# Two attention layers with mixtures of experts: PSUM banks dealt by head, and the products of an image's step spread anew

## The reference

```python
x = x + tanh(g_xattn[0]) * L0_xattn(layernorm(x), ctx, Wq, bq, Wk, bk, Wv, bv, Wo, bo)
x = x + tanh(g_ffn[0])   * L0_ffn(layernorm(x), ...)      # 32 experts, 4 per row, and a shared one
x = x + tanh(g_xattn[1]) * L1_xattn(layernorm(x), ctx, ctx, gamma)
x = x + tanh(g_ffn[1])   * L1_ffn(layernorm(x), ...)      # 8 experts, 2 per row, and shared ones

def L0_xattn(x, c, ...):        # 16 heads of 8 channels; layer 1 has 8 heads of 16
    q, k, v = Wq x + bq, Wk c + bk, Wv c + bv
    p = softmax(einsum('bhkt,bhks->bhts', q, k) / sqrt(8), axis=-1)
    return Wo einsum('bhts,bhks->bhkt', p, v) + bo
```

## Time and profile before

| | |
|---|---|
| median of 3 runs | 734.75 us (732.73 to 735.25) |
| the profiled execution | 734.11 us, span 732.3 us |
| TensorE matmuls busy | 652.4 us, 89% of the span |
| VectorE busy | 517.6 us, 71% |
| ScalarE busy | 370.8 us, 51% |
| GpSimd busy | 355.1 us, 48% |
| mean granted clock of TensorE | 0.974 |
| layer 0 attention, roughly | 19 to 253 us of the span |
| layer 1 attention, roughly | 385 to 548 us |

### The profile page before, as it was taken

The page is one execution under the profiler, slowest core; times in us unless marked ns, Lnnn a source line. Parts: engine busy times, 40 slices in busy tenths (PEclk is TensorE's granted clock), DMA queues, the critical chain, the costliest instruction groups (busy, mean ns, idle before and its releaser), DMA issues.

```text
span 732.3 us, 13733 instructions
## 1 busy us (share of the span) xinstructions
PE 652.4 (89%) x4737; PEld 343.0 (47%) x4738; DVE 517.6 (71%) x1238; ACT 370.8 (51%) x616; POOL 355.1 (48%) x409
## 2 busy tenths in 40 slices
PE   3789999999999989989864778999989899999997
PEld 1233333333333336677541334445543367777754
DVE  3788989888889479946336898999873863333336
ACT  2147788788777634445330565666642203444430
POOL 3845646656431110077276886762010036777735
PEclk9999999999999999999995799999999999999999
DMA  6945545565633194044653667975317412222228
GB/s 149 211 108 137 147 124 140 151 177 148 171 95 88 46 308 82 6 150 139 192 166 96 190 202 194 231 208 157 109 40 235 118 33 70 87 89 88 68 95 282
DMA packets 110151, 101.12 MB, mean 138 GB/s; under 512 B 26344, under 2 KB 95629, under 8 KB 109611
## 3 DMA queue, kind: packets, MB, share of 16 engines
q1 hardware_dynamic: 100259, 80.52, 39.6%
q0 software_dynamic: 8352, 18.74, 9.1%
q10 hardware_dynamic: 1472, 0.99, 0.7%
HBM read 58.49 MB, written 24.40 MB: 113 GB/s over the span
## 4 chain that ended last, share of the span: by engine, by line
PE 58%; DVE 15%; issue 8%; POOL 7%; DMA 7%; SPq 3%; ACT 2%; POOLq 0%; ACTq 0%; DVEq 0%
PE O L478 12%; PE S L433 11%; PE ST L1569 6%; DVE mx L597 4%; POOL spare L305 4%; PE ST L441 3%; DMA QS<-mxT 3%; PE M L1586 2%; PE S L1586 2%; PE M L527 2%; PE M L520 2%; PE ST L1481 2%; SPq L170 1%; DMA PX<-xn,TI 1%; PE M L503 1%
## 5 line engine op out<-in xcount | busy, mean ns | idle before, releaser
L597 DVE TENSOR_REDUCE mx<-S 128x2 f32<-128x512 f32 x384 | 251.2, 684 | 37.0 <-PE S L433 35.1
L353 ACT ACTIVATE PX<-ST 128x1024 f32<-128x1024 f32 x192 | 196.1, 1023 | 95.3 <-PE ST L441 91.7
L433 PE MATMUL S<-QS 62*128 62x256 bf16 (+1 forms) x768 | 151.2, 292 | 37.0 <-DVE mx L597 29.0
L441 PE MATMUL ST<-QS 64*128 64x256 bf16 (+1 forms) x768 | 140.7, 277 | 4.5 <-DMA QS<-mxT 4.5
L478 PE MATMUL O<-PX,VA 128*32 128x256 f32 x1536 | 122.7, 392 | 0.1
L433 PEld LDWEIGHTS S<-QS 62*128 62x128 bf16 (+1 forms) x768 | 48.5, 97 | 153.9 <-DVE mx L597 98.7
L305 POOL DMA_INDIRECT spare<-ye,GI x64 | 68.2, 1066 | 26.4 <-issue 12.6
L1687 POOL DMA_INDIRECT PX<-xn,TI x39 | 39.8, 1020 | 52.6 <-DVE K1n L1881 37.2
L441 PEld LDWEIGHTS ST<-QS 64*128 64x128 bf16 (+1 forms) x768 | 53.8, 96 | 19.0 <-issue 9.0
L810 POOL DMA_INDIRECT PX<-xn,TI x32 | 34.1, 1065 | 53.6 <-DVE spare L1196 44.1
L284 POOL TENSOR_TENSOR X<-X,rd 128x256 f32<-128x256 f32 x16 | 11.6, 726 | 86.0 <-ACT rd L363 86.0
(11 more groups left out here) (299 smaller groups left out, 1119.9 us busy)
## 6 DMA issues: line engine op xcount, KB each, us to landing
QS<-QKs SPq DMA_DIRECT2D x93, 128.0 KB
QS<-keys SPq DMA_DIRECT2D x16, 512.0 KB, 5.5
keys<-spare SPq DMA_DIRECT2D x96, 64.0 KB, 2.3
QS<-QKs SPq DMA_DIRECT2D x93, 64.0 KB
EGU<-in_ew SPq DMA_DIRECT2D x16, 256.0 KB, 4.4
xn<-spare SPq DMA_DIRECT2D x8, 512.0 KB, 10.9
ye<-QKc SPq DMA_DIRECT2D x32, 128.0 KB, 2.1
VA<-in_val SPq DMA_DIRECT2D x16, 256.0 KB, 3.7
```

Of the source, the lines that this page charges most:

```text
L353: e.activation(M["PX"][pair % 4][:, :], M["ST"][pair % 2][:, :], ACT.Exp, scale=A.scale).then_inc(A.exp, 1)
L433: got = e.matmul(M["S"][n % 2][:, 256 * a:256 * a + 256], QS[:, 0, 128 * a:128 * a + 128], QS[:, 1, :], start=True, stop=True)
L441: got = e.matmul(M["ST"][(NP * t + k // 2) % 2][:, 512 * u + 256 * a:512 * u + 256 * a + 256], QS[:, 1, 128 * a:128 * a + 128], QS[:, 0, : ...
L597: e.tensor_reduce(M["mx"][b % 2][:, :, A.row_of_max(head)], M["S"][n % 2][:, :].rearrange("p (a s) -> p a s", a=2), AX.X, ALU.max, negate= ...
```

## The change

Four things change together.

- PSUM: three banks S, three banks ST, each for one head; O and M1 stay. The waits follow: a score for a maximum may be three heads ahead instead of two, and exponentials are taken head by head.
- Layer 0, values: the two halves of a quad stand in one block, behind heads 4 (the last quad of the image before), 7, 11 and 14.
- Layer 0, other products and copies: projections behind head 2 (was 1), maxima's transposes behind 6 (was 5); on VectorE statistics at 2 (was 0), reciprocals at 4 (was 0), context's sum at 9 (was 10), normalisation at 12 (was 13); on ScalarE the copies move to the matching heads.
- In layer 1 the products stay in place; only banks and the exponentials' heads change.

```diff
+QK_OUT, MX_OUT, OS_FIRST, OS_LAST = 3, 6, 11, 4
...
-            w.wait_ge(A.st, A.NP * (b2 - U + 1))
+            w.wait_ge(A.st, H * (b2 - U + 1))
...
-    def exponentials(b, m):
-        pair = NP * b + m
-        w.wait_ge(A.st, pair + 1)
-
-        w.wait_ge(A.pv, pair // 2 - 1)
-        e.activation(M["PX"][pair % 4][:, :], M["ST"][pair % 2][:, :], ACT.Exp, scale=A.scale).then_inc(A.exp, 1)
+    def exponentials(b, k):
+        n = H * b + k
+        w.wait_ge(A.st, n + 1)
+
+        w.wait_ge(A.pv, n // 4 - 1)
+        e.activation(M["PX"][n // 2 % 4][:, 512 * (n % 2):512 * (n % 2) + 512], M["ST"][n % 3][:, :], ACT.Exp,
+                     scale=A.scale).then_inc(A.exp, 1)
...
-                if m == 0 and within(b0):
+                if k == QK_OUT and within(b0):
...
-                if m == 1 and within(b4):
+                if k == OS_LAST and within(b4):
                     values_out(b4, 1)
-                if m == 2 and within(b2):
+                if k == MX_OUT and within(b2):
                     rows_out(b2)
-                if m == 5 and within(b3):
+                if k == OS_FIRST and within(b3):
                     values_out(b3, 0)
...
-            w.wait_ge(A.max, n - 1)
+            w.wait_ge(A.max, n - 2)
...
-            w.wait_ge(A.exp, NP * t + k // 2 - 1)
+            w.wait_ge(A.exp, H * t + k - 2)
...
-                if k == 1 and within(b0):
+                if k == 2 and within(b0):
                     projections(b0)
-                if k in (2, 3) and within(b4):
-                    values(b4, 3, k - 2)
-                if k == 5 and within(b2):
+                if k == 4 and within(b4):
+                    values(b4, 3, 0, 1)
+                if k == 6 and within(b2):
                     maxima(b2)
-                if k in (6, 7, 10, 11, 14, 15) and within(b3):
-                    values(b3, k // 4 - 1, k % 2)
+                if k in (7, 11, 14) and within(b3):
+                    values(b3, (7, 11, 14).index(k), 0, 1)
...
-                if k == 0 and within(bn):
+                if k == (0 if t < 0 else 2) and within(bn):
                     statistics(bn)
...
-                if k == 0 and within(b5):
+                if k == 4 and within(b5):
                     reciprocals(b5)
-                if k == 10 and within(b2):
+                if k == 9 and within(b2):
...
-                if k == 13 and within(b5):
+                if k == 12 and within(b5):
                     normalized(b5)
...
-    S, ST = [ps("S0"), ps("S1")], [ps(f"ST{n}", 1024) for n in range(2)]
+    S, ST = [ps(f"S{n}") for n in range(3)], [ps(f"ST{n}") for n in range(3)]
     M["S"], M["ST"], M["O"], M["M1"] = S, ST, ps("O"), ps("M1")
-    M["BK"] = [S[0][:, :], S[1][:, :]] + [ST[n][:, 512 * k:512 * k + 512] for n in range(2) for k in range(2)]
-    M["BK"] += [M["O"][:, :], M["M1"][:, :]]
+    M["BK"] = [bank[:, :] for bank in S + ST + [M["O"], M["M1"]]]
```

More of the change, by code:

```diff
@@ L364, in attention_act @@
                          bias=M["bog"][:, 0:1], scale=M["tg"][:, 0:1]).then_inc(A.yb, 1)
-        for m in range(NP):
+        for k in range(H):
             if within(b3):
-                exponentials(b3, m)
+                exponentials(b3, k)
             if A.first:
-                if m == 0 and within(b0):
+                if k == QK_OUT and within(b0):
                     w.wait_ge(A.kp, b0 + 1)
@@ L376, in attention_act @@
                 if b0 == 0:
-                    if m == 1:
+                    if k == 4:
                         w.wait_ge(A.kc, 1)
                         e.activation(part_of(S, 0), Q, ACT.Copy).then_inc(A.cut0, 1)
-                    if m == 2:
+                    if k == 5:
                         w.wait_ge(A.res1, 1)
                         e.activation(part_of(S, 1), Q, ACT.Copy).then_inc(A.cut1, 1)
-                    if m == 3:
+                    if k == 6:
                         w.wait_ge(A.res2, 1)
-                        for k in range(3, 6):
-                            spread(e, A, M, 0, k)
-                if m == 1 and within(b4):
+                        for i in range(3, 6):
+                            spread(e, A, M, 0, i)
+                if k == OS_LAST and within(b4):
                     values_out(b4, 1)
-                if m == 2 and within(b2):
+                if k == MX_OUT and within(b2):
                     rows_out(b2)
-                if m == 5 and within(b3):
+                if k == OS_FIRST and within(b3):
                     values_out(b3, 0)
             else:
-                if m == 1:
+                if k == 3:
                     if within(b2):
@@ L402, in attention_act @@
                         e.activation(part_of(S, 0), Q, ACT.Copy).then_inc(A.cut0, 1)
-                if m == 2 and within(b0):
+                if k == 5 and within(b0):
                     w.wait_ge(A.res1, b0 + 1)
                     e.activation(part_of(S, 1), Q, ACT.Copy).then_inc(A.cut1, 1)
-                if m == 3 and b0 == 0:
+                if k == 7 and b0 == 0:
                     w.wait_ge(A.res2, 1)
-                    for k in range(3, 6):
-                        spread(e, A, M, 0, k)
-            meanwhile(t, m)
+                    for i in range(3, 6):
+                        spread(e, A, M, 0, i)
+            if k % 2:
+                meanwhile(t, k // 2)
 def attention_pe(e, w, A, M, meanwhile=lambda t, k: None):
-    H, NQ, NP = A.H, A.NQ, A.NP
+    H, NQ = A.H, A.NQ
     M1, QSs = M["M1"], M["QS" + A.name]
@@ L432, in for_maximum @@
             QS = QSs[A.stack(c)][row:row + A.K - 2, g, :, :]
[L433 removed]
+            got = e.matmul(M["S"][n % 3][:, 256 * a:256 * a + 256], QS[:, 0, 128 * a:128 * a + 128], QS[:, 1, :],
                            start=True, stop=True)
@@ L439, in for_exponential @@
             row, g = A.where(k)
-            QS, u = QSs[A.stack(t)][row:row + A.K, g, :, :], k % 2
-            got = e.matmul(M["ST"][(NP * t + k // 2) % 2][:, 512 * u + 256 * a:512 * u + 256 * a + 256],
+            QS = QSs[A.stack(t)][row:row + A.K, g, :, :]
+            got = e.matmul(M["ST"][(H * t + k) % 3][:, 256 * a:256 * a + 256],
                            QS[:, 1, 128 * a:128 * a + 128], QS[:, 0, :], start=True, stop=True)
-            if a and u:
+            if a:
                 got.then_inc(A.st, 1)
@@ L473, in values @@
         w.wait_ge(A.oe, n // 2)
-        w.wait_ge(A.exp, NP * b + 2 * quad + 2)
+        w.wait_ge(A.exp, H * b + 4 * quad + 4)
         for a in halves:
             for u in range(4):
-                pair = NP * b + 2 * quad + u // 2
+                pair = (H * b + 4 * quad + u) // 2
                 got = e.matmul(M["O"][32 * u:32 * u + 32, 256 * (quad % 2):256 * (quad % 2) + 256],
```

18 lines of the change are left out of this document (9 added, 9 removed).

## The result

The changed kernel takes 743.66 us (median of 4 runs, 741.79 to 746.62) where the kernel before takes 733.74 on the same chip (4 runs, 732.62 to 735.25): a ratio of 1.0152, interval 1.0118 to 1.0187. It is 9.9 us slower.

A forecast was written before the change was run, and what follows sets the result against it. The prediction took TensorE as the tightest engine, SyncE's queue just behind, and a loop through Cb to bind after the change: 734.1 - 1.5 + 13.0 - 5.0 - 1.0 = 739.6 us, range 733 to 747.

The forecast's parts named there:

- The loop through Cb: Layer 0, L505 to reciprocal, rT, SyncE's issues and Cb's landing: 14.8 us a round against 13.36, +13.0 over nine rounds.
- The queue does not bind (718): Rival, layer 0: the wait for rT does not hold Cb, TensorE's 12.4 sets the round; 718 us, chance 0.10.
- TensorE's own round: Layer 0: TensorE's work per image falls from 13.36 to 12.4 us through the blocks and the third bank.
- The banks: Layer 0, steady part: three banks for the maxima save 0.2 us an image of TensorE's waits.
- the blocks: Layer 0: a quad's values in one block instead of two save TensorE 0.76 us an image.
- Before the loop: Warm-up: with three banks TensorE bounds some 20 heads at 0.62 us each; 1.5 us saved.
- Exponentials by head, hidden: ScalarE, layer 0: +1.2 us an image, load 10.5 to 11.7, hidden by TensorE's 12.4; nothing taken.
- Behind the loop, -5.0: Last L505 to the end of layer 0's values, without Cb: blocks save 3.7, waits for maxima 1.3, together 5.0 us.
- Layer 1, -1.0: Layer 1, values not merged: the third bank saves 1.0 us, bounds 0 and 3.
- The clock falls in the new waits (746): Rival: TensorE's 2.4 us wait each round lowers the clock, some 0.7 a round, +6, 746 us; chance 0.11.
- The gains outweigh (733 to 737): Rival, no change: a loop of 14.4 costs 9.4, gains of 3 in layer 1 and 6 behind it; chance 0.12.

The follow-up runs named there:

- e1: The changed kernel with the reciprocals put back from behind head 4's maximum to behind head 0's: 726.47 us.
- e9: The kernel before with one edit, the next image's Cb issued ahead of the six stores of keys: 731.16 us.
- e5: The changed kernel with the reciprocals back behind head 0 and Cb issued ahead of the stores of keys: 717.55 us.
- e6: e5 with two of the six stores of keys issued by ScalarE instead of SyncE: 709.78 us.
- e4: The kernel before with only the new banks (three S, three ST) and exponentials by head, everything else where it was: 727.71 us.
- e10: e6 with the reciprocals moved back behind head 4, as the change has them: 729.86 us.
- e3: The changed kernel, reciprocals still behind head 4, with the next image's Cb issued ahead of the six stores of keys: 728.28 us.
- e11: The changed kernel with two of the six stores of keys issued by ScalarE, Cb in its old place: 731.37 us.
- e8: e3 with rT issued behind dn and on instead of between the parts of the spread: 726.48 us.
- e2: The kernel before with only the reciprocals moved, from behind head 0's maximum to behind head 4's: 770.62 us.
- e12: e10 with two buffers OS in layer 0, so a copy waits for the on<-OS of the image before the last: 718.12 us.
- e7: e4 with Cb issued ahead of the stores of keys: 720.21 us.

## Why the prediction was right, and where it was wrong

**The loop through Cb: right in place and size.** Forecast 14.8 us a round and +13.0; measured 14.88 and +13.7. L505 to the reciprocal was forecast at 0.52 + 0.43 + 1.20 + 0.35 = 2.50 and measured 2.61. SyncE needed 9.3 to 10.4 for a forecast of 9.8. The wait for Cb was to be "some 20 in all" and is 20.0. e1 shows that the one line makes it (17.2 us), and e9 that the kernel before was not held by the queue. The page of the Trainium skill that was set against it (DMA: Bandwidth & Descriptors, "Issuing engines are not separate DMA queues") has the sequencer's time as usually small. No trace here agrees: an issue takes some 0.60 us beside a landing of 2.1 to 2.3, 19 of them fill 11.5 us of each of SyncE's rounds, and moving two of them to ScalarE brought 7.8 us (e5 to e6).

**The queue does not bind (718): excluded** by the same runs. Even with the reciprocal at head 0 the changed kernel runs at 13.24, not 12.4 (e1), since the queue as it stands needs that much. TensorE's own round is 12.07 (e6); the prediction's 12.4 was 0.3 too long. The banks, with the exponentials by head, gave 0.43 where 0.2 was taken, and the blocks, with the other moves, 0.80 where 0.76 was.

**Before the loop:** forecast -1.5, measured -2.5.

**Exponentials by head, hidden: nothing speaks against it.** e4, which has them with the banks, is 6 us faster than the kernel before; one takes 594 ns.

**Behind the loop, -5.0: wrong, and the step that failed.** Measured +1.2. The forecast took this stretch to be free of the move, since no Cb is loaded. The prediction had named dn and on among what stands behind the waiting rT, but followed only Cb to the engine that needs it. The one that waits for on<-OS is ScalarE's copy. The waits of the changed kernel in this stretch, 201 to 265 us:

```profile
PEld O L483 <- ACT OS L348: 5.1, 7, 3.0
...
ACT OS L348 <- DMA on<-OS: 4.5, 2, 3.7
...
PE O L483 <- ACT OS L348: 2.7, 1, 2.7
```

The longest of them in the chain of work, 219 to 227 us, and the busy times and clock behind it:

```profile
219.53 0.60 SPq L243
220.18 3.76 DMA on<-OS
224.04 0.61 ACT OS L348
...
224.69 1.93 PE O L483 x16
```

```profile
223.80:230.40 6.60, 5.63 (x40) 2.21 (x42) 2.20 (x4) 4.69 (x10) 1.32 (x3) 0.50 0.25 63
```

on<-OS, which lands in 2.1 (median), took 3.76 here; the copy, the values and then TensorE waited; the granted clock fell to 0.50 for 6.6 us, and the block of 16 took 1.93 for 1.00. From this step's first block of values to the next step's are 16.4 us, in the two steps after it 11.6 and 11.5, the 11.5 forecast. rT was not held in this very step (issued at 216.95, the reciprocal had ended at 215.88). It is the rT of the step before that was late, 2.63 us behind its L510 (0.38 in the kernel before), and behind it SyncE issued without pause: dn went out 18.1 us behind the last L510, against 16.1. To these 2.0 the slow landing added 1.7. So the saving is there where the second loop does not close, and one step gave most of it back. e10 (60.2), e3 (62.6) and the changed kernel (63.4) all have the late reciprocal, and e1, e5 and e6 (58.7 to 59.1) do not; but e11 has it and takes 59.5, so that what it costs here hangs on how on<-OS lands in one or two steps. How much of 63.4 is the wait and how much the clock is not told apart. The term was too large besides: with the reciprocal at head 0 the stretch is 3.1 to 3.5 us shorter than before (e1, e5, e6), not 5.0.

**The drain between the layers: not foreseen.** The late reciprocal makes the last image's output 3.6 us later behind the last values. In the changed kernel the span up to layer 1 is 1.6 longer. That these are the drain's is likely and not shown: the span is 130.1 to 133.6 in the kernels with the reciprocal at head 0 and 134.0 to 135.9 in those with it at head 4 (139.9 in e8).

**Layer 1, -1.0:** measured -1.8, but the section is 157.4 to 161.8 over all kernels here, with edits that do not touch it, so nothing is shown by it.

**The clock falls in the new waits (746): a mechanism that is real, and not what decided.** In the changed kernel the clock is at 0.50 for 3.4 us at 83.8 and at 158.9, in two of the nine rounds, without lengthening the 2.61 from L510 to the reciprocal. In e2 waits of the same size brought it down in six of nine rounds, which are 1.7 to 2.6 us longer than the undisturbed 15.7: 12.8 us in all, about the gap between its forecast and its time. Of these 9.9 are in the stretch from L505 to the reciprocal; the rest is in SyncE's long issues and Cb's landings.

**The gains outweigh (733 to 737): no.** The loop was not shorter than forecast, and the gains behind it were not there.

The forecast of 739.6 stood 5.5 us above its base of 734.1, the measured medians stand 9.9 apart. Of the profiled difference of 12.5, the terms forecast with the loop (+13.0 - 1.5 - 1.0) account for 10.5 against 9.4 measured (+13.7 - 2.5 - 1.8). What is missing is the -5.0 behind the loop, which came out at +1.2, and the 1.6 up to layer 1. That the median of 743.66 lies inside 733 to 747 all the same is owed to the width of the range, which was set by the clock's rival and the loop's bounds and not by these two; the profiled execution, 746.62, lies just inside it.

## What to carry to other kernels

When an instruction that a DMA queue waits for is moved later, list every DMA behind the wait and follow each one to the engine that needs it or that needs its buffer back; here three paths ran through one waiting rT (Cb's landing, the reuse of OS, the drain), and opening the longest only uncovered the next. A queue that issues without pause is a bound like an engine's: add up its issues over a round and set the sum beside the busiest engine's before costing an edit that shortens that engine's work. A gain that is certain in busy time (here 1.2 us a round) arrives only when the loops through the queue are shorter than the new round, which one line, an earlier Cb and two stores moved to another queue decided between 743.66 and 709.78 us.

## What the runs showed of the hardware that was not expected

Now and then one issue on SyncE takes 0.9 to 2.1 us instead of 0.60, in every kernel here and at whichever DMA is then its turn (1.35 in the row of e12, 1.00 in the earlier trace rows). In the nine rounds there are 3 (e10) to 10 (the kernel before) of them, often some 12 us apart, and in the kernel before and in e5 they make SyncE's issues 0.65 to 0.68 us a round longer.

The landing of one and the same DMA spreads: on<-OS in 2.1 as a rule, 3.76 and 4.07 in the rounds that it spoilt (changed kernel, e3). Cb lands in 2.3 (median) in the changed kernel and in 2.8 (e5), 3.5 (e6) and 4.1 (e7) where it is issued ahead of the stores of keys. In a loop without slack each such case is a wait, and part of what an earlier issue wins is given back.

Which wait of TensorE takes the clock down does not follow from its length alone. Where the weights of the second projection waited for Cb in e2, the granted clock fell to 0.50 in or behind all seven waits of 2.25 to 3.61 us and at neither of 1.38 and 2.15. In the changed kernel it fell behind waits of 3.38 and 2.48, and stayed at 1.00 behind 2.45, 2.50 and 3.25. What else decides was not settled.
